# Two tables instead of three for ScalarE in a graph kernel's building stage, with two small numbers in one word

## What is computed

```
h = relu(layernorm(x)); x = x + attention(h, edges)        # softmax over each node's edges
h = relu(layernorm(x)); x = x + graph_conv(h, edges)       # normalised sum over edges, a product
h = relu(layernorm(x)); x = x + message_passing(h, edges)  # two MLPs on every edge, two sums
h = relu(layernorm(x)); x = x + gated_steps(h, edges)      # 4 GRU steps, 4 edge types
```

## Time and profile before

| | us |
|---|---|
| median of 3 runs | 17827.59 |
| range of the runs | 17825.18 to 17831.09 |
| the profiled execution | 17834.75 |
| its span (first to last instruction) | 17832.8 |

### The profile page before, as it was taken

How to read it: one execution, slowest core, us unless ns; L and a number is a source line. 1 busy time by engine, 2 the same in 40 slices (tenths; PEclk the granted TensorE clock), 3 DMA queues, 4 the chain that set the end, 5 groups by cost and what they waited for, 6 DMA issues and landing times.

```text
span 17832.8 us, 304910 instructions
## 1 busy us (share of the span) xinstructions
PE 11715.4 (66%) x67022; PEld 7505.4 (42%) x67023; DVE 6527.9 (37%) x30913; ACT 3403.6 (19%) x9727; POOL 6220.2 (35%) x6083
## 2 busy tenths in 40 slices
PE   2444444443455555567777776777766899999999
PEld 2222222221444444445555555555555444444443
DVE  6666666666333333333333333333333100000000
ACT  1333333333000000001222222222222000000000
POOL 2000000000445454515888888888884000000000
PEclk8555555555555555568999999999997899999999
DMA  2222222222111111143333333333335798989898
GB/s 92 76 79 79 79 79 79 78 80 85 40 34 35 34 35 34 35 174 77 42 42 42 42 42 42 42 41 42 42 42 44 270 341 333 342 331 342 332 342 309
DMA packets 1178112, 2116.60 MB, mean 119 GB/s; under 512 B 404316, under 2 KB 1020527, under 8 KB 1076671
## 3 DMA queue, kind: packets, MB, share of 16 engines
q1 hardware_dynamic: 828198, 1822.92, 29.2%
q0 software_dynamic: 348960, 284.02, 12.0%
HBM read 1647.55 MB, written 458.86 MB: 118 GB/s over the span
## 4 chain that ended last, share of the span: by engine, by line
PE 36%; issue 25%; POOL 14%; ACTq 11%; DVE 5%; another core or an unknown queue 3%; DMA 1%; ACT 1%; DVEq 1%; SPq 0%; POOLq 0%
PE ps L1350 12%; ACTq L781 11%; POOL G L465 7%; PE ps L1355 7%; POOL reverse L760 5%; PE ps L1066 4%; PE ps L1105 3%; PE ps L1095 2%; PE ps L1085 1%; DVE hots L1670 1%; PE ps L1292 1%; DMA reverse<-SD,sidx 1%; DVE hots L1669 1%; DVE hots L1668 1%
## 5 line engine op out<-in xcount | busy, mean ns | idle before, releaser
L1066 PE MATMUL ps<-hots 128*128 128x392 f16 x4859 | 1786.1, 478 | 2297.4 <-ACT stagebuf L795 1001.8
L760 POOL DMA_INDIRECT reverse<-SD,sidx x1660 | 2654.0, 1599 | 389.8 <-issue 378.8
L1350 PE MATMUL ps<-chunk,feat 128*128 128x512 f16 (+1 forms) x10192 | 2278.5, 375 | 14.4 <-DVE feat L1985 13.5
L463 POOL TENSOR_TENSOR hold_out<-hold_in 128x1 f32<-128x1 f32 x166 | 78.4, 472 | 5721.3 <-DMA kv_table<-big 4223.7
L1066 PEld LDWEIGHTS ps<-hots 128*128 128x128 f16 x4859 | 679.4, 140 | 3168.6 <-issue 3108.8
L795 ACT ACTIVATE stagebuf<-ps 128x392 f32 x3248 | 1377.7, 521 | 2737.4 <-issue 1749.8
L465 POOL DMA_INDIRECT G<-h_table,idx x1660 | 1653.6, 996 | 493.6 <-issue 489.4
L465 POOL DMA_INDIRECT G<-kv_table,idx x1660 | 1590.2, 958 | 518.0 <-issue 518.0
L1668 DVE TENSOR_SCALAR hots<-count_lo,key_lo 128x128 f16<-128x128 f16 x4859 | 1200.6, 247 | 1481.7 <-PE ps L1069 1479.9
L1839 DVE TENSOR_TENSOR acc<-acc,ps 128x132 f32 x1660 | 484.9, 292 | 3131.1 <-PE ps L1216 3045.8
L1213 PE MATMUL ps<-MS,OH 128*128 128x128 f32 x3320 | 783.1, 320 | 1259.1 <-issue 852.7
(11 more groups left out here) (391 smaller groups left out, 17812.7 us busy)
## 6 DMA issues: line engine op xcount, KB each, us to landing
chunk<-adj SPq DMA_DIRECT2D x720, 1792.0 KB, 8.9
adj<-stagebuf SPq DMA_DIRECT2D x406, 784.0 KB, 5.2
chunk<-adj SPq DMA_DIRECT2D x60, 1232.0 KB, 7.2
G<-in_edge SPq DMA_DIRECT2D x1660, 32.0 KB
G<-kv_table,idx POOLq DMA_INDIRECT x1660
G<-h_table,idx POOLq DMA_INDIRECT x1660
reverse<-SD,sidx POOLq DMA_INDIRECT x1660
reverse<-acc SPq DMA_DIRECT2D x4, 3225.0 KB, 20.0
```

What stands on the lines that cost most here:

```text
L760: nc.gpsimd.indirect_dma_start(reverse[j % R], bass.IndirectOffsetOnAxis(sidx[:, j:j + 1], 0), SD[:, j % R, :], None, compute_op=ALU.add). ...
L1066: nc.tensor.matmul(ps[:, bass.ds(held["to"][j % STEPW], 2 * COMBS)], hots[:, j % BRING, 0:P], hots[:, j % BRING, P:P + 2 * COMBS], start=F ...
L1350: nc.tensor.matmul(bank[k % 2][:, 0:cols], feat[0][:, hi, 0:2, :].rearrange("p a d -> p (a d)"), columns(chunk4, i % DRING, m, cols), star ...
```

## The change

The ring count (which slot use must be free, at most 207) and the offset `to` are put into one word: the count times 2^14, plus half the offset. So `virttab` has two rows, at partitions 32 and 64. ACT loads two tables a round, and for each eviction it shifts and masks the count out of the word, masks the offset out and doubles it. In the setup, DVE does one more small instruction and the transposed table has 52 rows instead of 78; SP sends one row less.

```diff
+RINGS = 1 << 14
...
-            table(1, virt_rows, 3, virttab, 32)
+            table(1, virt_rows, 2, virttab, 32)
...
             def evict(k, j, it):
-                if j % VIRTW == 0:
-                    held["end"], held["ring"] = words(32, k + 1, BSTEPS), words(64, k, NEV + EPRE)
-                    held["to"] = words(96, k, (SBUFS + OBUFS - 1) * SLEN + BLK - 2)
-                act.wait_ge(step_done, held["end"][j % VIRTW] & 8191)
-                act.wait_ge(events_done, held["ring"][j % VIRTW] & 255)
+                if j == 0:
+                    held["end"], held["ring_to"] = words(32, k + 1, BSTEPS), words(64, k, (NEV + EPRE + 1) * RINGS)
+                act.wait_ge(step_done, held["end"][j] & 8191)
+                act.wait_ge(events_done, (held["ring_to"][j] >> 14) & 255)
+                to = nc.s_assert_within(
+                    (held["ring_to"][j] & (RINGS - 1)) * 2, 0, (SBUFS + OBUFS - 1) * SLEN + BLK - 2,
...
                 nc.scalar.activation(
-                    stagebuf[:, bass.ds(held["to"][j % VIRTW], SLEN)].rearrange("p (x c) -> p x c", c=BLK)[:, :, 0:2],
+                    stagebuf[:, bass.ds(to, SLEN)].rearrange("p (x c) -> p x c", c=BLK)[:, :, 0:2],
...
-            turn_table(1, 3 * VC)
+            turn_table(1, 2 * VC)
...
-            link(scalar_(i1[:, V], i0[:, V], GRP - 1, 1, ALU.bitwise_and, ALU.arith_shift_left))
+            link(scalar_(i1[:, V], i0[:, V], GRP - 1, None, ALU.bitwise_and))
...
-            both_(out=tabcols[:, 2 * VC:3 * VC], in0=f3[:, V], scalar=float(SLEN), in1=i1[:, V], op0=ALU.mult, op1=ALU.add)\
+            link(both_(out=f3[:, V], in0=f3[:, V], scalar=float(SLEN // 2), in1=i1[:, V], op0=ALU.mult, op1=ALU.add))
+            both_(out=tabcols[:, VC:2 * VC], in0=ring, scalar=float(RINGS), in1=f3[:, V], op0=ALU.mult, op1=ALU.add)\
                 .then_inc(tab_cols, 1)
```

More of the change, by code:

```diff
@@ L164, in build @@
         step_rows = dram("step_rows", (3 * BC, P), I32)
-        virt_rows = dram("virt_rows", (3 * VC, P), I32)
+        virt_rows = dram("virt_rows", (2 * VC, P), I32)
         event_rows = dram("event_rows", (6, P), I32)
@@ L587, in _ @@
             table(0, step_rows, 3, steptab)
-            table(1, virt_rows, 3, virttab, 32)
+            table(1, virt_rows, 2, virttab, 32)
             table(2, event_rows, 3, eventtab)
-            sp.wait_ge(tab_loaded, 16 * 9)
+            sp.wait_ge(tab_loaded, 16 * 8)
             def keep(k, j, it):
@@ L777, in _ @@
                 nc.scalar.activation(key_hi[:, lo:lo + n * P], bank[2 + q % 2][:, 0:n * P], ACT.Copy).then_inc(key_copied, 1)
-            act.wait_ge(tab_loaded, 16 * 9)
+            act.wait_ge(tab_loaded, 16 * 8)
             def words(row, k, top):
@@ L782, in words @@
                     virttab[row:row + 1, k:k + VIRTW] if known(k) else virttab[row:row + 1, bass.ds(k, VIRTW)], engines=(act.engine,),
-                    min_val=0 if row == 96 else 1, max_val=top,
+                    min_val=1, max_val=top,
                     skip_runtime_bounds_check_because="the path's tables are made of counts within these bounds")
@@ L789, in evict @@
             def evict(k, j, it):
-                if j % VIRTW == 0:
-                    held["end"], held["ring"] = words(32, k + 1, BSTEPS), words(64, k, NEV + EPRE)
-                    held["to"] = words(96, k, (SBUFS + OBUFS - 1) * SLEN + BLK - 2)
-                act.wait_ge(step_done, held["end"][j % VIRTW] & 8191)
-                act.wait_ge(events_done, held["ring"][j % VIRTW] & 255)
+                if j == 0:
[4 more added lines that the diff above has]
+                    (held["ring_to"][j] & (RINGS - 1)) * 2, 0, (SBUFS + OBUFS - 1) * SLEN + BLK - 2,
+                    skip_runtime_bounds_check_because="the path's tables are made of counts within these bounds")
                 nc.scalar.activation(
-                    stagebuf[:, bass.ds(held["to"][j % VIRTW], SLEN)].rearrange("p (x c) -> p x c", c=BLK)[:, :, 0:2],
+                    stagebuf[:, bass.ds(to, SLEN)].rearrange("p (x c) -> p x c", c=BLK)[:, :, 0:2],
                     bank[j % 8][:, 0:2 * COMBS].rearrange("p (x c) -> p x c", c=2), ACT.Copy).then_inc(evicted, 1)
-            pipeline(act, VW, 16, 0, lambda it, j: stage(VW, 16, it, j, 0, evict))
+            pipeline(act, VW, VIRTW, 0, lambda it, j: stage(VW, VIRTW, it, j, 0, evict))
             root(1)
@@ L1042, in _ @@
                 last.then_inc(key_turned, 1)
-            pe.wait_ge(tab_loaded, 16 * 9)
+            pe.wait_ge(tab_loaded, 16 * 8)
             pe.wait_ge(key_copied, 10)
@@ L1592, in _ @@
             link(scalar_(f3[:, V], bank[5][:, VC:2 * VC], float(EPRE - SBUFS + 1), None, ALU.add))
-            link(both_(out=tabcols[:, VC:2 * VC], in0=over_, scalar=float(SBUFS - OBUFS), in1=f3[:, V], op0=ALU.mult, op1=ALU.add))
+            ring = f4[:, V]
+            link(both_(out=ring, in0=over_, scalar=float(SBUFS - OBUFS), in1=f3[:, V], op0=ALU.mult, op1=ALU.add))
             link(tensor_(f3[:, V], extra, regular, ALU.subtract))
@@ L1614, in _ @@
             v.wait_ge(tab_stored, 16)
-            copy_(tabi[0:3 * VC, :], bank[7][0:3 * VC, 0:P]).then_inc(tab_copied, 1)
+            copy_(tabi[0:2 * VC, :], bank[7][0:2 * VC, 0:P]).then_inc(tab_copied, 1)
             v.wait_ge(cmp_used, 3 * CG + VC)
```

## The result

The changed kernel takes 17651.77 us (17648.2 to 17656.62), the kernel before 17829.34 us. The ratio is 0.9901, with a 95% interval of 0.9884 to 0.9918. The forecast was 17,681 us with a range of 17,620 to 17,790: the way and the range hold, and the gain is 178 us where 147 were expected.

The account below looks back on a forecast made before the run. ACT's three register loads, 9.4 us of each 20.2 us building round, were taken to be on the path. -228 + 61 + 4 + 16 = -147 us from 17827.6 gave 17,681 us, range 17,620 to 17,790.

Parts of the forecast that it names:

- The third load: Building stage, ACT's path: dropping the third table's load and address row saves 1.13 us a round, 228 us over 202 rounds.
- the bound by the second load's 1.19 us: Upper bound for the removed table in ACT's loop: 1.29 us a round with address row and pauses, 261 us in all.
- The first load unchanged: ACT's first load each round in the building stage: held up by the slot's transfer, it keeps its 7.1 us.
- a table is worth a third of all loads: Larger gain: each table in ACT's loop is worth 3.10 us, so 562 us saved, 17,266 us; chance 2%.
- the sum by 200 ns a register: ACT's removed load at 200 ns a register: 3.2 us for 16 words, about -590 us; the prediction did not use it.
- Two register instructions, exposed twice a round: ACT's evictions: 0.15 us more each, exposed at a round's 16th and first after the loads; 61 us, plus 4 for others.
- What doesn't come through: Building stage: rounds where PE's late loads leave DVE's ring not full give back a tenth of the saving, 16 us.
- The other three: Building stage terms: third load -228 us, exposed register instructions +61 us, the other evictions' register instructions +4 us.
- What PE waits for: Building stage: PE's waits for ACT stay near 197 in number and fall by about 0.8 us each.
- The slower rival: ACT's sequencer sets the pace, exposing the addition at all 16 evictions: +1.27 us a round, +257 us, 18,084 us; 7%.

## Why the prediction was right, step by step

- **The third load.** -228 us expected. Put back, the load alone was worth 204 us; with the 16 us that its address row takes in the chain, which no run tested, 220. The row 1.03 us for the third load was the right one; the bound by the second load's 1.19 us was not needed.
- **The first load unchanged.** Held (7.02 us, not 7.11), and the reason is now shown: with half as many bytes again it takes 2.0 us more, away from the transfer 3.4 us less. The rival "a table is worth a third of all loads", 3.1 us, falls. So does the sum by 200 ns a register: 16 words cost 1.03 us here. The Trainium skill (Runtime: NRT & Kernel Launch, instruction fetch mechanics) states that figure for the register loads which the runtime adds around a kernel, and these come from HBM; the prediction set it against loads out of SBUF, to which it need not apply.
- **Two register instructions, exposed twice a round.** 61 + 4 us of loss expected, 58 measured, on the same footing as the 220. The burst's pitch stayed 0.39 us.
- **What doesn't come through.** This is the term that was most in error: 16 us expected, on no row. The other three, -228 + 65, are -163 us, and the stage gave -162. That it is so near has luck in it: 10 us of the third load did not come through, and the register instructions cost 7 less than reckoned. Both are little more than two profiles of one kernel differ by.
- **What PE waits for.** That its waits for ACT would stay 197 and take the whole saving did not hold: 217 waits, 105 us less of them, and 43 us less of waiting for DVE.
- **The rest of the difference** of 31 us between 147 and 178: 15 us are in the stage, the others lie behind it, 14 of them in an attention pass that differs from chip to chip. The prediction had the stages behind keep their lengths; on the one chip where both kernels were profiled, all that follows the stage is 7 us shorter after the change.
- **The slower rival** had its mechanism right and its place wrong: the sequencer does overtake the engine, at two more instructions, but then only about 4 of 16 evictions are exposed, not 7.5 or 16.

## What to carry to other kernels

A register load by a sequencer is no small thing next to engine work of half a microsecond: look for it by its own line in the chain, and count loads apart from words. What it costs depends on what runs beside it: with the loop begun at the ninth eviction the two loads that were left gave another 283 us (461 - 178), more than the removal of the third; before a load is removed, see whether a transfer holds it. And ask what the next engine does in a gap before it is shortened: the move by 12 evictions took 3.5 us off ACT's gap and gave 1.0 us a round, since PE's own pauses grew, with two tables and with three alike, while 1.1 us of load gave nearly all of itself in either place.

## What the runs showed of the hardware that was not expected

- A load of 16 words by ACT's sequencer took 1.19 us as the second and 1.03 us as the third of a series, whichever row it read, and 3.6 us as the first, with no transfer beside it. What the first one waits for is open. It took 3.64 us ahead of the stage too, right behind other ACTIVATEs, so it does not belong to the evictions; and it is no rule for every engine, since PE's loads of 4 and 8 words took at most 1.18 us with no transfer beside them, the first of a series included.
- A transfer of 1.57 MB out of SBUF held the first load until about its end (7.0 us), and with 2.35 MB 9.1 us. PE's loads in the same time took up to 3.9 us, in place of 0.6 to 1.2. SP's three loads of one word for each slot all ran beside a transfer and took 0.9 to 1.4 us in the kernel before; the only three without one, ahead of the stage, took 0.27 to 0.46.
- PE's loads of 8 words took 0.59 and 0.76 us, by place, and the same two with 16 words 1.11 and 1.28: eight words more cost 0.5 us in both.
- The same program's attention pass took 3,178, 3,194 and 2,189 us on three chips, within 3 us alike for all kernels profiled on one of them. In the shorter one the DMA engines were busy for 23% of it in place of 16%; the cause lies outside the program and is open. Ratios of such kernels should come from one chip.
